# Scores' factor by exp(-2 ln) of the summed norms, with joined row and head copies, in an attention and expert kernel

## The chip, the cores and the metric

The kernel runs on one core of a Trainium2 chip. The metric is the device time of one execution in microseconds. Before the change it is 966.4 us in the median of three runs (966.29 to 967.87).

## The reference

The input is 32 sequences of 128 tokens with 256 features, and a context of the same shape. There are 16 heads of 16 features. After a layer norm, attention against the context comes with an unusual score, and then a second layer norm and a top-2 mixture of 8 experts with 1024 hidden features:

```python
scores = jnp.einsum('bhqd,bhkd->bhqk', qh, kh)
norm_q = jnp.linalg.norm(qh, axis=-1)
norm_k = jnp.linalg.norm(kh, axis=-1)
D_udps = (norm_q[..., :, None] + norm_k[..., None, :]) ** 2
D_safe = jnp.where(D_udps == 0.0, jnp.inf, D_udps)
scores = alpha * 4.0 * scores / D_safe
attn = jax.nn.softmax(scores, axis=-1)
...
logits = jnp.einsum('btd,de->bte', x, Wr)
w, idx = jax.lax.top_k(jax.nn.softmax(logits, axis=-1), 2)
h = jax.nn.gelu(jnp.einsum('btd,edh->ebth', x, W1) + b1[:, None, None, :], approximate=False)
y = jnp.einsum('ebth,ehd->ebtd', h, W2) + b2[:, None, None, :]
out = jnp.einsum('ebtd,bte->btd', y, dispatch)
```

For each query and key of each head the score is divided by the square of the sum of the two norms. With lq and lk the logarithms of the norms, and q', k' the unit vectors, 4 q.k / (nq + nk)^2 equals (q'.k') (1 - tanh^2((lq - lk) / 2)). The kernel before uses this form. The changed kernel computes exp(-2 ln((nq + nk) / scale)) and multiplies the raw q.k with it.

## The kernel before, in words

All five engines have programs written out by hand, with semaphores between them; no scheduler moves anything. Attention works on pairs of sequences, 16 pairs (`NP`). The loop of each engine is a software pipeline over `it`: while pair `it` gets its scores, pair `it + 1` is projected and its norms are made, pair `it + 2` is normalised, and pair `it - 1` is projected out and routed. Each pair has four factor steps n = 0 to 3: sequence b = n // 2 and half of the heads h = n % 2, so 8 heads, 1024 columns.

For one pair the work around the change is this:

1. TensorE projects q and k into a bank; ScalarE squares it (`squares`, L789) and copies it out (L792), then copies v (L781).
2. VectorE sums the squares over each head (L1060) and splits the sums in mantissa and exponent (`mantissas`, L1067 to L1070). ScalarE takes Ln (`norm_ln`, L796), VectorE forms the logarithm of the norms, with a sign, and splits it in three bf16 parts (`logarithms`, L1078 to L1092). ScalarE takes Exp (`norm_exp`, L800) and VectorE makes the unit vectors' coefficients (`unit_coefficients`, L1096 to L1102).
3. TensorE transposes the parts (`rows`, L433). VectorE copies them to `aq` and `kbr` (L1111, L1114), and SyncE writes the key rows by six small transfers into one row each of `uk` (`flat_rows`, L308).
4. POOL scales q and k to unit vectors (`units`, L1501, L1505), TensorE transposes them (`stack`) and ScalarE copies them out (L806, L809).
5. `factors(n)`: a matmul of `aq` and `uk` gives the sum for 128 x 1024 (L473), ScalarE applies Tanh (L817) and Square (L819). `scores(n)`: TensorE makes q.k (L485), VectorE multiplies by the factor (L1124) and takes the maximum (L1130).
6. `turned(n, i)`: TensorE transposes the product (L495) and subtracts the maximum by eight matmuls (L502), ScalarE takes the softmax's Exp (L827), and `values(n)` (L519) is the last step.

Three PSUM banks (`gen`) are handed round by the list `TURNS`: each use takes the bank that was used three places earlier, and waits until that use's reader has released it. So `wsum`, the sum of a weight's squares (L585, then L1283), takes the bank that the first exponential of n = 1 (`ex10`) has read, and `ex20` takes that of `wsum`. A factor's matmul needs that ScalarE has read the factor before, since there is one `u_ps`.

Meanwhile the expert weights are loaded and split (`weight_high` L862, `weight_low` L1277), and every second pair's tokens are routed and scattered (L1517). After the last pair come 71 slots of 128 tokens through the experts (L711, L928, L1375, L1377, L729).

ScalarE evaluates functions from a table that is loaded in sets. The build puts an instruction ACT_TABLE_LOAD ahead of an activation whose function is not in the set that is loaded; it is attributed to that activation's line.

Of the kernel before, what the change touches and what calls it, by code (L numbers as in the profile page):

```python
# [12 lines left out]
P = 128  # L13
# [19 lines left out]
QK_SCALE = 2.0 ** 12  # L33
# [7 lines left out]
    "dve_norms": ["mant", "ah", "parts", "coef"],  # L41
# [37 lines left out]
def build(nc, ctx, io):  # L79
# [119 lines left out]
    with ExitStack() as a:  # L199
# [19 lines left out]
        colscale = alloc(a, "colscale", [P, 2 * NH], F32)  # L219
        signs = alloc(a, "signs", [P, 2 * NH], F32)  # L220
# [11 lines left out]
        na = {k: alloc(a, f"na_{k}", [P, 2, 2 * NH], I32 if k in ("mant", "ex") else F32)  # L232
              for k in ("mant", "ex", "exf", "ln", "ah", "y", "y2", "n2y2", "rn", "coef", "r1", "r2")}
        ar = alloc(a, "ar", [P, 2, 2, RROWS], BF16)
        kbr = pair(a, "kbr", [RROWS, P], BF16)
# [3 lines left out]
        aq = pair(a, "aq", [RROWS + NSPLIT, P], BF16)  # L239
        uk = pair(a, "uk", [RROWS + NSPLIT, NH * P], BF16)  # L240
# [10 lines left out]
        wkk = alloc(a, "wkk", [P, 1], I32)  # L251
# [19 lines left out]
        def sync_program(sp):  # L271
# [125 lines left out]
        def tensor_program(pe):  # L397
# [49 lines left out]
            def stack(b, p):  # L447
                pe.wait_ge(*at("unit", p + 1))
# [13 lines left out]
            def factors(n, p):  # L462
# [300 lines left out]
        def scalar_program(act):  # L763
# [20 lines left out]
            def squares(b, p):  # L784
# [5 lines left out]
                if p:  # L790
                    act.wait_ge(*at("unit", p))
# [20 lines left out]
            def factors(n, p):  # L812
# [52 lines left out]
            for it in range(-1, NP + 3):  # L865
# [17 lines left out]
                if 0 <= it < NP:  # L883
                    norm_exp(it)
# [65 lines left out]
        def vector_program(dve):  # L950
# [31 lines left out]
            def set_scales():  # L982
# [10 lines left out]
                dve.tensor_scalar(escale[:, :], abig[:, :].bitcast(F32), QK_SCALE ** -2, None, ALU.mult).then_inc(sig("set_a"), 1)  # L993
                dve.memset(signs[:, 0:NH], 1.0)
# [645 lines left out]
```

## Time and profile before

| what | value |
|---|---|
| median of the runs | 966.4 us |
| the profiled execution, its own time | 970.74 us |
| its span on the core | 968.9 us |
| mean granted TensorE clock | 0.977 |
| PE busy, PEld busy | 898.1 us (93%), 789.8 us (82%) |
| DVE busy | 697.2 us (72%) |
| ACT busy | 634.5 us (65%) |
| POOL busy | 415.5 us (43%) |

PE is TensorE's matmuls, PEld its weight loads, DVE is VectorE, ACT is ScalarE, POOL is GpSimd, SP is SyncE. Idle is what a view puts ahead of an instruction, with the instruction that ended it behind an arrow. A group of the view by line has the number of instructions, their busy time in us, the mean of one in ns, and the idle time ahead of them. The granted clock is a share of TensorE's full 2.4 GHz, so 0.50 is 1.2 GHz. A stretch of time is given from the start of the span.

### The profile page before, as it was taken

The numbers are of one execution on the slowest core, as the hardware profiler recorded it, in microseconds if no ns is written. First come the engines' busy times: TensorE is split into PE (matmuls) and PEld (weight loads), VectorE is DVE, ScalarE is ACT, GpSimd is POOL, SyncE is SP. The second block draws the span as 40 slices with busy tenths as digits, with TensorE's granted clock in tenths as the row PEclk, the third lists the DMA queues.
The fourth block names the chain that finished last, engine by engine and source line by source line (L and its number), as shares of the span: only waits on it lengthen the run. The fifth ranks groups of instructions, "written<-read, shape, count | busy, mean of one in ns | idle before, by whom it ended". The sixth has DMA issues, their size and how long they took to land.

```text
span 968.9 us, 30634 instructions
## 1 busy us (share of the span) xinstructions
PE 898.1 (93%) x10701; PEld 789.8 (82%) x10701; DVE 697.2 (72%) x1833; ACT 634.5 (65%) x1236; POOL 415.5 (43%) x540
## 2 busy tenths in 40 slices
PE   3999999998999999989899699899999999999994
PEld 2788887787877877878777589799999999999993
DVE  7677888777987887779768577766666666666662
ACT  3688887787877877878857356455555455554551
POOL 6344456538546565385253532623222232222322
PEclk9799999999999999999979799999999999999998
DMA  5222122314132333253044773443333233332222
GB/s 150 70 72 89 41 83 80 112 41 128 57 99 76 126 123 103 92 171 111 20 139 134 275 273 52 85 93 52 51 52 51 47 52 52 52 51 48 46 30 22
DMA packets 61892, 84.82 MB, mean 88 GB/s; under 512 B 9872, under 2 KB 55312, under 8 KB 59568
## 3 DMA queue, kind: packets, MB, share of 16 engines
q1 hardware_dynamic: 47504, 64.26, 21.0%
q0 software_dynamic: 13296, 18.00, 11.1%
q8 instruction: 91, 1.49, 0.6%
q10 hardware_dynamic: 944, 0.60, 0.2%
q14 instruction: 57, 0.47, 0.2%
HBM read 49.86 MB, written 31.92 MB: 84 GB/s over the span
## 4 chain that ended last, share of the span: by engine, by line
PE 74%; issue 7%; DVE 6%; ACT 6%; POOL 3%; another core or an unknown queue 1%; DMA 1%; DVEq 0%; POOLq 0%; ACTq 0%
PE s_ps L711 10%; PE u_ps L711 10%; PE pv_ps L729 9%; PE gen L729 9%; PE gen L502 5%; PE gen L495 5%; PE s_ps L485 5%; PE u_ps L473 3%; PE pv_ps L519 2%; PE gen L544 2%; ACT pt L827 2%; PE gen L415 2%; PE gen L680 2%; PE gen L418 2%; PE gen L422 1%
## 5 line engine op out<-in xcount | busy, mean ns | idle before, releaser
L1567 POOL DMA_INDIRECT out<-yw,rb x71 | 110.3, 1553 | 269.4 <-DVE yw L1392 253.4
L928 ACT ACTIVATE h<-s_ps,b1t,inv 128x128 f32<-128x128 f32 x288 | 107.8, 457 | 89.6 <-PE s_ps L711 79.3
L928 ACT ACTIVATE h<-u_ps,b1t,inv 128x128 f32<-128x128 f32 x280 | 104.7, 459 | 87.4 <-PE u_ps L711 86.4
L1375 DVE TENSOR_SCALAR hs<-h,hsc 128x512 f16<-128x512 f32 x142 | 69.7, 491 | 120.4 <-ACT h L928 102.0
L827 ACT ACTIVATE pt<-gen,escale 128x512 f32<-128x512 f32 x128 | 86.8, 686 | 50.4 <-PE gen L502 34.5
L1377 DVE SCALAR_TENSOR_TENSOR hs<-h,hsc,hs 128x512 f16<-128x512 f32 x142 | 106.7, 751 | 5.1
L711 PE MATMUL s_ps<-xt,w1s 128*128 128x128 f16 x1728 | 104.8, 220 | 2.2 <-issue 2.2
L1517 POOL DMA_INDIRECT xrec<-rec,idx x64 | 77.8, 1215 | 60.9 <-DVE idx L1229 44.7
L711 PE MATMUL u_ps<-xt,w1s 128*128 128x128 f16 x1680 | 102.5, 220 | 0.9 <-issue 0.9
L711 PEld LDWEIGHTS s_ps<-xt,w1s 128*128 x1728 | 99.8, 99 | 2.8 <-issue 2.3
L729 PE MATMUL pv_ps<-w2s_sb,hs 128*128 x864 | 100.5, 272 | 0.5 <-issue 0.5
L711 PEld LDWEIGHTS u_ps<-xt,w1s 128*128 x1680 | 97.2, 99 | 2.0 <-issue 1.5
L1124 DVE SCALAR_TENSOR_TENSOR tw<-th,s_ps 128x1024 f32<-128x1024 f32 x64 | 77.9, 1217 | 27.2 <-PE s_ps L485 21.9
L729 PE MATMUL gen<-w2s_sb,hs 128*128 x840 | 97.4, 273 | 0.0
L729 PEld LDWEIGHTS pv_ps<-w2s_sb,hs 128*128 128x128 f16 x864 | 82.5, 98 | 11.0 <-issue 1.5
L495 PE MATMUL gen<-idf,tw 128*128 128x128 f32 x512 | 79.5, 278 | 10.7 <-DVE wcl L1283 7.9
L502 PE MATMUL gen<-negb,mhl 128*128 128x128 bf16 x1024 | 79.2, 220 | 9.7 <-POOL mhl L1488 9.3
L729 PEld LDWEIGHTS gen<-w2s_sb,hs 128*128 128x128 f16 x840 | 80.9, 98 | 8.8
L1130 DVE TENSOR_REDUCE tm<-tw 128x8 f32<-128x1024 f32 x64 | 78.1, 1220 | 2.2
L817 ACT ACTIVATE th<-u_ps 128x1024 f32<-128x1024 f32 x64 | 65.6, 1026 | 20.5 <-PE u_ps L473 20.3
L502 PEld LDWEIGHTS gen<-negb,mhl 128*128 128x128 bf16 x1024 | 67.9, 99 | 13.6 <-POOL mhl L1488 11.6
L485 PE MATMUL s_ps<-kt,qt 32*128 32x128 f32 x1024 | 75.6, 286 | 0.9 <-DVE tw L1124 0.9
(251 smaller groups left out, 1741.8 us busy)
## 6 DMA issues: line engine op xcount, KB each, us to landing
wl<-L_ffn_W SPq DMA_DIRECT2D x16, 1024.0 KB
rb<-xrec SPq DMA_DIRECT2D x71, 132.5 KB
w2s<-wst SPq DMA_DIRECT2D x8, 1024.0 KB
w2s_sb<-w2s SPq DMA_DIRECT2D x8, 1024.0 KB, 20.4
xin<-x SPq DMA_DIRECT2D x32, 128.0 KB, 3.5
cin<-ctx SPq DMA_DIRECT2D x32, 128.0 KB, 2.1
xres<-x SPq DMA_DIRECT2D x32, 128.0 KB
out<-x SPq DMA_DIRECT2D x30, 128.0 KB, 2.0
```

The lines of the kernel that those rows point to most:

```text
L485: ins = pe.matmul(s_ps[:, i, j * P:(j + 1) * P], qt[b][rws, j // 2, :], kt[b][rws, j // 2, j % 2, :], start=True, stop=True)
L495: pe.matmul(g[:, j * P:(j + 1) * P], tw[h][:, i, j, :], idf[:, :], is_transpose=True, start=(j == 0), stop=False)
L502: ins = pe.matmul(g[:, j * P:(j + 1) * P], m, negb[:, :], start=False, stop=(j == 3 and part == 1))
L711: ins = pe.matmul(hbank[n % HBANKS][:, o:o + SLOT], w, xt[s % 2][:, xp, k, :], start=(t == 0), stop=(t == len(terms) - 1))
L729: ins = pe.matmul(y, hs[s % 3][:, hp, m, :], w, start=(m == 0 and t == 0), stop=(m == HC - 1 and t == 2))
L827: act.activation(pt[n % 2][:, i, :], turn(f"ex{n}{i}", p)[:, :], ACT.Exp, scale=escale[:, :]).then_inc(sig(f"ex{n}{i}"), 1)
L928: ins = act.activation(h32[n % HBANKS][:, m % HB, :], hbank[n % HBANKS][:, o:o + SLOT], ACT.Gelu, scale=inv1[:, bass.ds(ex, 1)].bitcast(F3 ...
L1124: dve.scalar_tensor_tensor(tw[h][:, :, :, :].rearrange("p i j k -> p (i j k)"), th[h][:, :], -1.0, s_ps[:, :, :].rearrange("p i k -> p (i ...
L1130: dve.tensor_reduce(tm[h][:, :], tw[h][:, :, :, :].rearrange("p i j k -> p (i j) k"), AX.X, ALU.max).then_inc(sig(f"tm{n}"), 1)
L1377: dve.scalar_tensor_tensor(lo, h, scale, hi, ALU.mult, ALU.subtract).then_inc(sig("lo"), 1)
L1517: pool.indirect_dma_start(xrec_d[:, :], bass.IndirectOffsetOnAxis(ap=idx[:, i, t:t + 1], axis=0), rec[m % 2][:, t, :], None).then_inc(sig( ...
L1567: pool.indirect_dma_start(out[:, :], bass.IndirectOffsetOnAxis(ap=rb[j][:, D + NE:D + NE + 1], axis=0), yw[s % 2][:, :], None, compute_op= ...
```

## The change

The factor is made another way, and some copies are joined.

- `norm_ln` and `norm_exp` become `roots`: ScalarE takes Ln of the sums of squares with a small bias, and Exp of -0.5 times that right behind, which gives 1/norm. VectorE corrects it by a Newton step and forms the norm itself (`norms`), which it splits in three parts. Mantissas, signs and unit coefficients are gone.
- `factors`: Tanh becomes Ln (new line L822), and Square becomes Exp with scale -2 and a bias tile (L824).
- `units`: POOL multiplies q by a constant per head and copies k, with a wait for q and k alone and one signal for each sequence.
- `scores` on VectorE multiplies without the -1.
- `aq`, `kbr` and `uk` hold both sequences of a pair; two copies take the place of four, and one semaphore counts all six row transfers. The first factor of a pair waits for all six.
- `heads_back` makes one product instead of two, and `weight_exponent` writes in place.

The core of the diff:

```diff
@@ flat_rows (SP)
-                for b in range(2):
-                    sp.wait_ge(*at(f"rowk{b}", p + 1))
-                    if p:
-                        sp.wait_ge(*at(f"su{2 * b + 1}", p))
-                    for s in range(NSPLIT):
...
+                sp.wait_ge(*at("rowk", p + 1))
+                if p:
+                    sp.wait_ge(*at("u3", p))
+                for s in range(NSPLIT):
+                    for b in range(2):
...
@@ factors (PE)
-                pe.wait_ge(*at(f"rowq{b}", p + 1))
-                pe.wait_ge(*dma(f"flat{b}", NSPLIT * (p + 1)))
+                if n == 0:
+                    pe.wait_ge(*at("rowq", p + 1))
+                    pe.wait_ge(*dma("flat", 2 * NSPLIT * (p + 1)))
@@ scalar_program
-            def norm_ln(p):
-                act.wait_ge(*at("mant", p + 1))
-                act.activation(na["ln"][:, :, :], na["mant"][:, :, :].bitcast(F32), ACT.Ln).then_inc(sig("nln"), 1)
-
-            def norm_exp(p):
-                act.wait_ge(*at("ah", p + 1))
-                act.activation(na["y"][:, :, :], na["ah"][:, :, :], ACT.Exp, scale=-1.0).then_inc(sig("ny"), 1)
+            def roots(p):
+                for b in range(2):
+                    act.wait_ge(*at(f"n2{b}", p + 1))
...
+                act.activation(na["ln"][:, :, :], n2[:, :, :], ACT.Ln, bias=tiny[:, :]).then_inc(sig("nln"), 1)
+                act.wait_ge(*at("nln", p + 1))
+                act.activation(na["y"][:, :, :], na["ln"][:, :, :], ACT.Exp, scale=-0.5).then_inc(sig("ny"), 1)
...
-                act.activation(th[h][:, :], u_ps[:, :], ACT.Tanh, scale=0.5).then_inc(sig(f"th{n}"), 1)
+                act.activation(th[h][:, :], u_ps[:, :], ACT.Ln, scale=-0.5 / NORM_SCALE).then_inc(sig(f"th{n}"), 1)
                 act.wait_ge(*at(f"th{n}", p + 1))
-                act.activation(th[h][:, :], th[h][:, :], ACT.Square).then_inc(sig(f"t2{n}"), 1)
+                act.activation(th[h][:, :], th[h][:, :], ACT.Exp, scale=-2.0, bias=centre[:, :]).then_inc(sig(f"t2{n}"), 1)
@@ vector_program, norms (new; mantissas, logarithms, unit_coefficients are removed)
+            def norms(p):
+                dve.wait_ge(*at("ny", p + 1))
+                step(dve.tensor_tensor(na["y2"][:, :, :], na["y"][:, :, :], na["y"][:, :, :], ALU.mult))
+                step(dve.scalar_tensor_tensor(na["n2y2"][:, :, :], n2[:, :, :], TINY, na["y2"][:, :, :],
+                                              ALU.max, ALU.mult))
+                step(dve.scalar_tensor_tensor(na["rn"][:, :, :], na["n2y2"][:, :, :], -3.0, na["y"][:, :, :],
+                                              ALU.add, ALU.mult))
+                step(dve.scalar_tensor_tensor(na["r1"][:, :, :], n2[:, :, :], TINY, na["rn"][:, :, :],
+                                              ALU.max, ALU.mult))
...
@@ rows (DVE)
+                dve.tensor_copy(kbr[:, :, :], both[:, :, 1, :]).then_inc(sig("rowk"), 1)
...
+                dve.tensor_copy(aq[0:RROWS, :, :], both[:, :, 0, :]).then_inc(sig("rowq"), 1)
@@ scores (DVE)
-                dve.scalar_tensor_tensor(tw[h][:, :, :, :].rearrange("p i j k -> p (i j k)"), th[h][:, :], -1.0,
...
+                dve.tensor_tensor(tw[h][:, :, :, :].rearrange("p i j k -> p (i j k)"), th[h][:, :],
+                                  s_ps[:, :, :].rearrange("p i k -> p (i k)"), ALU.mult).then_inc(sig(f"tw{n}"), 1)
@@ units (POOL)
-                pool.wait_ge(*at("coef", p + 1))
...
+                pool.wait_ge(*at(f"qke{b}", p + 1))
...
+                pool.tensor_tensor(qu[b][:, :, :], qk[:, b, 0:NH, :],
+                                   colscale[:, :].unsqueeze(2).to_broadcast([P, NH, DK]), ALU.mult)
+                for odd in range(2):
+                    ins = pool.tensor_copy(ku[b][:, :, odd, :, odd, :],
+                                           qk[:, b, NH + odd:2 * NH:2, :].rearrange("p (k g) d -> p k g d", k=2))
@@ the orders
 ACT:   squares(0), v_out(0), roots (was norm_ln), turned(1, 0), [norm_exp], turned(1, 1)
 DVE:   squares(0), [mantissas], weight_diagonal, logits(0), norms (was logarithms), weight_exponent, [unit_coefficients], rows
```

On ACT, from the factors of n = 2 and 3 over the norms to the first softmax exponential of n = 1, the order is before (`th` is the factor, `pt` the exponentials, `vz` v, `na_ln` and `na_y` the norms' Ln and Exp):

```order
L817 ACTIVATE th<-u_ps 128x1024
L819 ACTIVATE th<-th 128x1024
L817 ACTIVATE th<-u_ps 128x1024
L819 ACTIVATE th<-th 128x1024
L789 ACTIVATE qk<-gen 128x512
L792 ACTIVATE qk<-gen 128x512
L781 ACTIVATE vz<-gen 128x16x16
L796 ACT_TABLE_LOAD
L796 ACTIVATE na_ln<-na_mant 128x64
L827 ACT_TABLE_LOAD
L827 ACTIVATE pt<-gen,escale 128x512
L800 ACTIVATE na_y<-na_ah 128x64
```

and from the factor of n = 3 on it is after:

```order
L822 ACT_TABLE_LOAD
L822 ACTIVATE th<-u_ps 128x1024
L824 ACT_TABLE_LOAD
L824 ACTIVATE th<-th,centre 128x1024
L791 ACTIVATE qk<-gen 128x512
L794 ACTIVATE qk<-gen 128x512
L783 ACTIVATE vz<-gen 128x16x16
L803 ACT_TABLE_LOAD
L803 ACTIVATE na_ln<-n,tiny 128x64
L805 ACT_TABLE_LOAD
L805 ACTIVATE na_y<-na_ln 128x64
L832 ACTIVATE pt<-gen,escale 128x512 x2
```

Each Ln and each Exp of a factor has a table load ahead of it, and the norms' Exp has moved ahead of the exponential. Over the whole program 36 table loads stand on ACT before, and 164 after.

On DVE, behind the sums of squares, the order is before (`wdg`, `wss` and `wcl` belong to the weight's exponent, `ar` are the three parts):

```order
L1266 TENSOR_TENSOR wdg<-gen,idf 128x128
L1270 TENSOR_REDUCE wss<-wdg 128x1
L1162 TENSOR_SCALAR r_l<-gen 128x8
L1078 SCALAR_TENSOR_TENSOR na_ah<-na_ln,na_exf 128x64
L1084 TENSOR_TENSOR na_r<-na_ah,signs 128x64
L1088 CAST ar<-na_r 128x4x16
L1089 TENSOR_TENSOR na_r<-na_r,ar 128x64
L1090 CAST ar<-na_r 128x4x16
L1091 TENSOR_TENSOR na_r<-na_r,ar 128x64
L1092 CAST ar<-na_r 128x4x16
L1283 TENSOR_SCALAR wcl<-gen 128x1
```

and after:

```order
L1242 TENSOR_TENSOR wdg<-gen,idf 128x128
L1246 TENSOR_REDUCE wss<-wdg 128x1
L1138 TENSOR_SCALAR r_l<-gen 128x8
L1067 TENSOR_TENSOR na_y<-na_y 128x64
L1068 SCALAR_TENSOR_TENSOR na_n2y<-n,na_y 128x64
L1070 SCALAR_TENSOR_TENSOR na_rn<-na_n2y,na_y 128x64
L1072 SCALAR_TENSOR_TENSOR na_r<-n,na_rn 128x64
L1078 CAST ar<-na_r 128x4x16
L1079 TENSOR_TENSOR na_r<-na_r,ar 128x64
L1080 CAST ar<-na_r 128x4x16
L1081 TENSOR_TENSOR na_r<-na_r,ar 128x64
L1082 CAST ar<-na_r 128x4x16
```

The chain from ScalarE's result to the last part has nine instructions instead of seven, and what it waits for is the Exp, not the Ln.

## Rows read from the trace of the kernel before

**Rows 1.** The page, part 1: busy time and its share of the span.
```profile
PE 898.1 (93%) x10701; PEld 789.8 (82%) x10701; DVE 697.2 (72%) x1833; ACT 634.5 (65%) x1236; POOL 415.5 (43%) x540
```

**Rows 2.** First and last pair, and pair 14: L817 in order of time.
```profile
31.06 1.02 ACT L817 ACTIVATE th<-u_ps 128x1024 f32<-128x1024 f32 x1 [0.26 <-PE u_ps L473]
...
481.98 1.02 ACT L817 ACTIVATE th<-u_ps 128x1024 f32<-128x1024 f32 x1 [0.64 <-PE u_ps L473]
...
493.04 1.02 ACT L817 ACTIVATE th<-u_ps 128x1024 f32<-128x1024 f32 x1 [0.32 <-PE u_ps L473]
...
513.77 1.04 ACT L817 ACTIVATE th<-u_ps 128x1024 f32<-128x1024 f32 x1
```

**Rows 3.** Stretch 166 to 463 us: PE, PEld, DVE, ACT, POOL, granted clock, DMA.
```profile
166.00:463.00 297.00, 278.85 (x3035) 233.07 (x3033) 239.31 (x705) 240.04 (x382) 173.16 (x260) 1.00 0.31 102
```

**Rows 4.** Waits, 166 to 463 us: total, times, longest.
```profile
...
ACT pt L827 <- remote: 14.4, 5, 2.9
...
ACT pt L827 <- PE gen L502: 13.7, 30, 1.2
...
ACT th L817 <- PE u_ps L473: 11.1, 19, 0.9
...
```

**Rows 5.** Groups of ACT: count | busy us, mean ns | idle before.
```profile
L827 ACT ACTIVATE pt<-gen,escale 128x512 f32<-128x512 f32 x128 | 86.8, 686 | 50.4 <-PE gen L502 34.5 <-remote 14.4
...
L819 ACT ACTIVATE th<-th 128x1024 f32<-128x1024 f32 x64 | 67.7, 1058 | 2.0
...
L796 ACT ACT_TABLE_LOAD x16 | 20.5, 1283 | 0.3
...
L827 ACT ACT_TABLE_LOAD x15 | 19.2, 1283 | 0.3
...
L834 ACT ACTIVATE osb<-pv_ps 128x512 f32<-128x512 f32 x32 | 19.1, 598 | 1.9 <-PE pv_ps L519 0.3
```

**Rows 6.** Order of time on ACT: start, duration, line, tiles, [idle before].
```profile
250.32 1.04 ACT L817 ACTIVATE th<-u_ps 128x1024 f32<-128x1024 f32 x1
...
261.35 1.02 ACT L817 ACTIVATE th<-u_ps 128x1024 f32<-128x1024 f32 x1
262.41 1.06 ACT L819 ACTIVATE th<-th 128x1024 f32<-128x1024 f32 x1
...
266.73 0.38 ACT L781 ACTIVATE vz<-gen 128x256 f32<-128x256 f32 x1
267.13 1.28 ACT L796 ACT_TABLE_LOAD   x1
268.43 0.26 ACT L796 ACTIVATE na_ln<-na_mant 128x64 f32<-128x64 f32 x1
268.70 1.28 ACT L827 ACT_TABLE_LOAD   x1
270.00 0.69 ACT L827 ACTIVATE pt<-gen,escale 128x512 f32<-128x512 f32 x1
...
272.10 0.69 ACT L827 ACTIVATE pt<-gen,escale 128x512 f32<-128x512 f32 x1 [1.18 <-PE gen L502]
```

**Rows 7.** Groups of DVE and PE that stand in the norms' chain.
```profile
L1102 DVE TENSOR_TENSOR na_coef<-na_rn,colscale 128x64 f32<-128x64 f32 x16 | 3.6, 225 | 0.5
...
L585 PE MATMUL gen<-wss,ones_f 128*128 128x1 f32 x32 | 6.1, 260 | 4.8 <-ACT pt L827 3.1 <-issue 1.7
```

**Rows 8.** The SP queue: issues of six row copies of one pair.
```profile
243.49 3.67 SPq L308 DMA_DIRECT2D uk<-kbr  x6
```

**Rows 9.** PE after its idle times, in order of time.
```profile
24.96 0.66 PE L433 MATMUL gen<-idb,ar 128*96 128x128 bf16 x4 [4.09 <-DVE ar L1092]
...
40.48 1.49 PE L485 MATMUL s_ps<-kt,qt 32*128 32x128 f32 x16 [0.95 <-DVE tw L1124]
```

**Rows 10.** Stretches of 3 us: PE busy first, granted clock after POOL.
```profile
27.00:30.00 3.00, 3.00 (x14) 2.40 (x13) 1.90 (x7) 1.15 (x3) 1.57 (x4) 0.50 0.04 7
...
42.00:45.00 3.00, 3.00 (x9) 2.04 (x9) 2.44 (x2) 2.00 (x2) 0.45 (x3) 0.57 0.00 0
```

More of the change, by code:

```diff
@@ L32 @@
 X_SCALE = 2.0 ** 11
-QK_SCALE = 2.0 ** 12
+TINY = 1e-37
+NORM_SCALE = 4.0
+CENTRE = 2.0
 ONE = 1 << 23
@@ L231, in build @@
         n2 = alloc(a, "n2", [P, 2, 2 * NH], F32)
[L232 to L233 removed]
+        na = {k: alloc(a, f"na_{k}", [P, 2, 2 * NH], F32)
+              for k in ("ln", "y", "y2", "n2y2", "rn", "r1", "r2")}
         ar = alloc(a, "ar", [P, 2, 2, RROWS], BF16)
[L235 removed]
+        kbr = alloc(a, "kbr", [RROWS, 2, P], BF16)
         qt, kt = pair(a, "qt", [P, 2, P], F32), pair(a, "kt", [P, 2, 2, P], F32)
[L239 to L240 removed]
+        aq = alloc(a, "aq", [RROWS + NSPLIT, 2, P], BF16)
+        uk = alloc(a, "uk", [RROWS + NSPLIT, 2, NH * P], BF16)
         vz = pair(a, "vz", [P, 2, NH, VC], F32)
@@ L447, in stack @@
             def stack(b, p):
-                pe.wait_ge(*at("unit", p + 1))
+                pe.wait_ge(*at(f"un{b}", p + 1))
                 g = pe_turn(pe, f"qte{b}", p)
@@ L1090, in logarithms @@
+                step(dve.tensor_tensor(v4(na["r2"]), v4(na["r1"]), part(0), ALU.subtract))
                 step(dve.tensor_copy(part(1), v4(na["r2"])))
[L1091 to L1103 removed]
@@ L1105, in rows @@
-            def rows(p):
-                gb = turn("rows_t", p)[:, :].bitcast(BF16)
-                dve.wait_ge(*at("rows_t", p + 1))
-                for b in range(2):
-                    if p:
-                        dve.wait_ge(*at(f"su{2 * b + 1}", p))
-                    dve.tensor_copy(aq[b][0:RROWS, :], gb[0:RROWS, 2 * b * P:(2 * b + 1) * P]).then_inc(sig(f"rowq{b}"), 1)
-                    if p:
-                        dve.wait_ge(*dma(f"flat{b}", NSPLIT * p))
-                    dve.tensor_copy(kbr[b][:, :], gb[0:RROWS, (2 * b + 1) * P:(2 * b + 2) * P]).then_inc(sig(f"rowk{b}"), 1)
+                step(dve.tensor_tensor(v4(na["r1"]), v4(na["r2"]), part(1), ALU.subtract))
@@ new lines, in norms, with rows @@
+                dve.tensor_copy(part(2), v4(na["r1"])).then_inc(sig("parts"), 1)
+            def rows(p):
+                gb = turn("rows_t", p)[:, :].bitcast(BF16)[:, 0:4 * P]
+                dve.wait_ge(*at("rows_t", p + 1))
+                both = gb[0:RROWS, :].rearrange("r (b i t) -> r b i t", b=2, i=2)[:, :, :, :]
+                if p:
+                    dve.wait_ge(*dma("flat", 2 * NSPLIT * p))
+                dve.tensor_copy(kbr[:, :, :], both[:, :, 1, :]).then_inc(sig("rowk"), 1)
+                if p:
+                    dve.wait_ge(*at("u3", p))
+                dve.tensor_copy(aq[0:RROWS, :, :], both[:, :, 0, :]).then_inc(sig("rowq"), 1)
@@ L1284, in weight_exponent @@
                 dve.wait_ge(*at("wcl", p + 1))
-                exponent(wcl[:, :], wkk[:, :])
-                dve.tensor_copy(dst[:, p % NE:p % NE + 1], wkk[:, :])
-                dve.tensor_scalar(wsc[:, :], wkk[:, :], -float(ONE), 268.0 * ONE, ALU.mult, ALU.add).then_inc(sig("wsc"), 1)
+                place = dst[:, p % NE:p % NE + 1]
+                exponent(wcl[:, :], place)
+                dve.tensor_scalar(wsc[:, :], place, -float(ONE), 268.0 * ONE, ALU.mult, ALU.add).then_inc(sig("wsc"), 1)
             for it in range(-2, NP + 3):
@@ L1325, in vector_program @@
                 if 0 <= it + 1 < NP:
-                    logarithms(it + 1)
+                    norms(it + 1)
                 if 0 <= it < NP:
```

117 lines of the change are left out of this document (36 added, 81 removed), and 2 rows, old and new, of the table TURNS.

## The prediction

> **What bounds the kernel now.** I read the page's busy line first: TensorE (PE) is busy for 93% of the span [rows 1], but that is a mean over two stages, attention over 16 pairs and then the experts, and the change touches only attention. So next a window over the middle of attention. Two L817 rows frame the stage: the first factor of the first pair starts at 31.06 us and that of the last at 513.77 [rows 2], so 15 pairs take 482.7 us, 32.2 each. In the window of 297 us PE is busy 278.9, ScalarE (ACT) 240.0, VectorE (DVE) 239.3, GpSimd (POOL) 173.2 [rows 3]. Per pair of 32.3 us in that window (9.2 pairs) that is PE 30.3, ACT 26.1, DVE 26.0. PE paces, and ACT is second with only 6.2 us of idle per pair. Then the waits of ACT: it waits on PE in small pieces, 13.7 us in 30 pieces before the softmax exponentials, 11.1 us in 19 before the factors, and 14.4 us in 5 pieces of up to 2.9 that the trace puts to an unnamed releaser [rows 4]. ACT and PE run in lockstep, each waiting a little for the other; what is added to ACT beyond some 4 to 6 us a pair must lengthen the pair.
>
> **The change, part by part.** *Table loads.* This decides. The built order shows an ACT_TABLE_LOAD ahead of every Ln and every Exp that alternate. Before, Tanh, Square and Exp follow one another with none, and only the norms' Ln is framed by two. Now each of the four factors of a pair has two (one ahead of Ln, one ahead of Exp), and the norms keep two: 10 a pair where there were 2. Over the program 164 stand where 36 did, 128 more. One takes 1283 ns, each of the 31 in the two groups of the attention stage alike [rows 5]. What one adds to the queue is a little more. From vz at 266.73 to the exponential at 270.00 are 3.27 us with two loads and one 0.26 us Ln in between [rows 6]; without loads, with engines' overlap, I put these starts 0.43 apart, so 1.42 per load where it breaks an overlap. Tanh to Square, which depends on it, stands 1.06 apart (261.35, 262.41) for 1.02 of work [rows 6], so no overlap is lost there: 1.30. Per pair 4 x 1.42 + 4 x 1.30 = 10.9 us.
>
> The Trainium skill (ScalarE: Activation LUTs, What ACT_TABLE_LOAD costs) says that a switch costs the 1283 ns load and about 1380 ns of drain, some 2.66 us in total. By that page the 128 loads would add 340 us and the time would be near 1290. The row disagrees: Ln starts 1.30 us after its load [rows 6], so the load's length agrees and the drain is not there to be seen.
>
> *Activations.* Tanh becomes Ln with the same shape, Square becomes Exp; I charge equal time, as nothing in the rows separates functions. But the new Exp reads its bias from a tile. 128x512 with a per-partition operand takes 686 ns (L827), the same size without one 598 (L834) [rows 5]: 0.09 more. Five such per pair (four Exp, the norms' Ln) make 0.4. So ACT gets 11.3 us more a pair: 26.1 + 11.3 = 37.4, above PE's 30.3. ACT becomes the engine that paces.
>
> *What ACT still waits for.* Waits that come from PE being late vanish, since PE works through the 2.6 us that each factor now takes longer. Round trips stay. After the norms' Exp comes the first exponential of factor 1, then PE's weight sum (its bank is freed by just that exponential), eight matmuls and the second. Today the two start 2.10 apart (270.00, 272.10) [rows 6] with small work between that moves away: about 1.5 idle. In every second pair the unnamed wait of 2.9 stands in its place [rows 4], 0.8 more on the mean. Four later hand-overs keep some 0.8 in all (estimated from the 13.7 us in 30 pieces), two new small ones, ahead of factor 1 and ahead of factor 2's exponentials, 0.6. Sum 3.7, and 37.4 + 3.7 = 41.1 us a pair.
>
> *TensorE's clock.* PE will idle 10 us a pair. The longest piece is new: PE finishes the projection and waits with the weight products for ACT to empty the q k bank behind factors 2 and 3, about 4 us. In this trace PE idle for 4.09 us ahead of 24.96 [rows 9] is followed by a granted clock of 0.50, that is 1.2 of 2.4 GHz, while PE is fully busy [rows 10]; after a wait of 0.95 at 40.48 [rows 9] it falls as well, to a mean of 0.57 [rows 10]. Cold, the scores, values and transposes behind the wait double: between nothing (hidden behind the norms' loads) and 2.9 us a pair (weight products 0.9, scores 1.1 and values 0.6 are hidden in part, two groups of 0.9 are not). I take 0.9. Pair: 42.0 us.
>
> *The norms on DVE.* Removed are three mantissa steps, the sum, the sign and the unit coefficient; added are the clamped ones. The part that leads to the row copies grows from seven to nine instructions of 225 ns [rows 7] and now starts after two loads instead of one. Both stand in the shadow of the round trip just counted; where the cover is gone they cost at most 0.5 + 1.5 a pair. The wait that is added on DVE (for the norms' Exp) has the weight exponent, the row copies and factor 3's product queued behind it, and PE waits for the exponent to free a bank: 0.3 of the 0.6 above is that. Ahead of the first pair nothing covers it: +1.9 once.
>
> *POOL, joined copies, joined products.* POOL no longer waits for coefficients; it has 13 us of slack a pair [rows 3], and stack is early by that but waits for a bank anyway: 0. Two DVE copies in place of four, one product in place of two, one copy less in the weight exponent: between 0 and -0.6 a pair, on an engine off the path: 0. The new product of factor and scores keeps its 1024 columns: 0. The first factor now waits for all six row transfers instead of three; six are issued in 3.67 us, done at 247.16 [rows 8], while that pair's first factor runs at 250.32 [rows 6]: 0, and 1.8 if that cover went (half of the 3.67).
>
> **The sum.** 15 pairs at 42.0 are 630; the first four have no routing work and are 0.8 shorter each, 627. Against 482.7: +144. The last pair has its eight loads and 0.4 of bias, less 2.4 of waits that vanish: +8.5. Start +1.9. In pair 14 factor 2 runs 11.1 after factor 1 (481.98 to 493.04) [rows 2] where others need 4.5, while DVE makes tables; with ACT pacing I count 4 of that back. The expert stage has the same instructions: 0. Total +151, on the profiled execution's 970.7 (span 968.9) 1121; that execution is 4.3 above the median of 966.4, so 1117. As the waits are the weaker part and my estimates of them are rounded upward, I forecast **1115**.
>
> **The rivals.**
> *ACT's idle swallows it.* Nearly all waits go, 1.5 a pair left, and the clock costs nothing: 38.9 a pair, 583 + 7, +108: 1075. For it: 6.2 idle per pair today, all waits on PE. Against it: the round trip through the weight sum cannot be filled, as ACT's order is fixed.
> *The clock falls in each pair at the worst place.* 2.9 a pair instead of 0.9: +30 more, and if DVE's cover goes as well, another 0.5 a pair: about 1150. For it: the 0.95 us wait was already followed by the lower clock. Against: the clock is 1.00 over the whole window of today, its PE idle of 2 us a pair (18.1 of 297 us) notwithstanding [rows 3].
> *The loads do not appear: not slower.* Mechanism: Ln and Exp served by one set, so that the loads at the norms go too. ACT then loses 2 x 1.42 and gains 0.4, 23.7 a pair; PE's 30.3 is the floor, so at most 1.9 x 15 = 28 us are gained: about 940 to 955. It decides if the profile after has fewer than 36 loads. Against it: the built order shows all 164. The Trainium skill (ScalarE: Activation LUTs, Table sets: the hidden batching unit) states such a set, natural_log_exp_and_others, and one load for Ln then Exp; the trace of before has separate loads for Ln and Exp [rows 6], which speaks for two sets here too.
> *Each switch costs the drain as well* (from 128 x 2.7, about 1290): 1%; the start of Ln right behind its load excludes it.
>
> **How the numbers follow.** Forecast with its own range 1095 to 1130: 0.64. Swallowed, 1060 to 1095: 0.17. Clock and more, 1130 to 1165: 0.15. No loads, 940 to 955: 0.03. Drain: 0.01. The range that leaves out no more than 2 in 10 is 1080 to 1140. Its low end is nearly the floor without clock, its high end the forecast with about 1.7 a pair more. A difference of 0.2% (1.9 us) can be told here. Faster 0.025, within 0.005, slower 0.97.
>
> **What would show it.** 164 ACT_TABLE_LOAD of 1283 ns; ACT busy near 37 us a pair, idle under 5, PE at 30 busy of 40 to 42; first factor of the last pair near 31 + 2 + 627 = 660; th pairs, L822 to L824, 2.3 apart; dips of PEclk in attention; the end of the span some 455 us after the last pair's first factor, as now. Wrong would be: a pair under 38.9 (waits), over 44 (clock or DVE's chain), table loads that are shorter or missing, or Ln over 1024 columns unlike Tanh's 1.02.

## The result, and the profile after

| | time, us | ratio to before | 95% interval |
|---|---|---|---|
| before | 967.0 (966.3 to 967.9) | | |
| changed | 1121.7 (1118.8 to 1124.2) | 1.160 | 1.157 to 1.163 |

The change makes the kernel 154.7 us slower. The forecast was 1115, with a range of 1080 to 1140. The profiled execution took 1123.9 us, with a span of 1122.1.

The page of the changed kernel, part 1 and the line of the granted clock in part 2 (tenths, in 40 slices):

```profile
PE 966.5 (86%) x10701; PEld 839.9 (75%) x10701; DVE 679.4 (61%) x1672; ACT 802.9 (72%) x1364; POOL 407.8 (36%) x540
...
PEclk8688998998988998998988988899999999999998
```

TensorE falls from 93% to 86% of a longer span [rows 1], and ScalarE goes from 634.5 us busy to 802.9, which is 168.4 more. 128 loads of 1.283 us are 164.2 of that. The clock line has an 8 or less in about every second slice of the attention stage, its first 25 slices. Next the groups of ScalarE, which answer to [rows 5]:

```profile
L832 ACT ACTIVATE pt<-gen,escale 128x512 f32<-128x512 f32 x128 | 85.5, 681 | 70.5 <-PE gen L504 69.1
L822 ACT ACT_TABLE_LOAD x64 | 82.1, 1283 | 1.1
L824 ACT ACT_TABLE_LOAD x64 | 82.1, 1283 | 1.1
L824 ACT ACTIVATE th<-th,centre 128x1024 f32<-128x1024 f32 x64 | 73.5, 1148 | 0.8
L822 ACT ACTIVATE th<-u_ps 128x1024 f32<-128x1024 f32 x64 | 65.5, 1024 | 0.7
L803 ACT ACT_TABLE_LOAD x16 | 20.5, 1283 | 0.3
L805 ACT ACT_TABLE_LOAD x16 | 20.5, 1283 | 0.3
...
L803 ACT ACTIVATE na_ln<-n,tiny 128x64 f32<-128x64 f32 x16 | 5.6, 347 | 0.2
```

Every load takes the 1283 ns of before. Ln over 1024 columns takes 1024 ns where Tanh took 1.02 us; Exp with its bias tile takes 1148 where Square took 1058, 0.09 more. The norms' Ln takes 347 with its bias tile and took 0.26 us without one ([rows 6]), the same 0.09. The first factor of the first pair and that of the last pair, which answer to [rows 2]:

```profile
31.97 1.02 ACT L822 ACTIVATE th<-u_ps 128x1024 f32<-128x1024 f32 x1
```
```profile
660.66 1.02 ACT L822 ACTIVATE th<-u_ps 128x1024 f32<-128x1024 f32 x1
```

15 pairs take 628.7 us instead of 482.7, that is 41.9 a pair instead of 32.2. This is 146.0 of the 153.2 us by which the span is longer. Ahead of them 0.9 are lost (the start moves from 31.06 to 31.97), behind them 6.3 (from the last pair's first factor to the end it was 455.1 us and is 461.4).

One pair of ScalarE in order of time, from the factor of n = 2 on, to be laid beside [rows 6]:

```profile
378.57 1.28 ACT L822 ACT_TABLE_LOAD   x1
379.86 1.02 ACT L822 ACTIVATE th<-u_ps 128x1024 f32<-128x1024 f32 x1
380.90 1.28 ACT L824 ACT_TABLE_LOAD   x1
382.20 1.15 ACT L824 ACTIVATE th<-th,centre 128x1024 f32<-128x1024 f32 x1
383.36 1.28 ACT L822 ACT_TABLE_LOAD   x1
384.66 1.02 ACT L822 ACTIVATE th<-u_ps 128x1024 f32<-128x1024 f32 x1
385.70 1.28 ACT L824 ACT_TABLE_LOAD   x1
386.99 1.15 ACT L824 ACTIVATE th<-th,centre 128x1024 f32<-128x1024 f32 x1
388.05 0.58 ACT L791 ACTIVATE qk<-gen 128x512 f32<-128x512 f32 x1
388.52 0.59 ACT L794 ACTIVATE qk<-gen 128x512 f32<-128x512 f32 x1
389.00 0.38 ACT L783 ACTIVATE vz<-gen 128x256 f32<-128x256 f32 x1
389.40 1.28 ACT L803 ACT_TABLE_LOAD   x1
390.70 0.35 ACT L803 ACTIVATE na_ln<-n,tiny 128x64 f32<-128x64 f32 x1
391.06 1.28 ACT L805 ACT_TABLE_LOAD   x1
392.36 0.26 ACT L805 ACTIVATE na_y<-na_ln 128x64 f32<-128x64 f32 x1
392.52 0.67 ACT L832 ACTIVATE pt<-gen,escale 128x512 f32<-128x512 f32 x1
396.81 0.69 ACT L832 ACTIVATE pt<-gen,escale 128x512 f32<-128x512 f32 x1 [3.62 <-PE gen L504]
```

From the first load to the end of v the engine never waits. Ln to Exp is 2.34 us here (379.86 to 382.20), where Tanh to Square was 1.06; the factor of n = 2 to that of n = 3 is 4.80 where it was 2.41 (261.35 to 263.76). The one long wait is the last row: 3.62 us ahead of the second exponential of n = 1, where it was 1.18, or 2.9 in pairs with routing. What TensorE does meanwhile:

```profile
389.25 1.44 PE L581 MATMUL gen<-wl 128*128 128x128 bf16 x16 [4.02 <-ACT qk L794]
...
391.38 2.08 PE L487 MATMUL s_ps<-kt,qt 32*128 32x128 f32 x16
393.39 1.08 PE L521 MATMUL pv_ps<-pt,vz 128*32 128x128 f32 x16
...
394.85 1.09 PE L497 MATMUL gen<-idf,tw 128*128 128x128 f32 x4
395.74 1.03 PE L504 MATMUL gen<-negb,mhl 128*128 128x128 bf16 x8
```

and the stretches of 3 us around it (PE, PEld, DVE, ACT and POOL busy, then the granted clock):

```profile
386.00:389.00 3.00, 0.00 (x0) 0.00 (x0) 0.34 (x1) 2.99 (x4) 2.02 (x4) 1.00 0.82 258
389.00:392.00 3.00, 2.75 (x26) 2.75 (x28) 1.09 (x4) 2.95 (x5) 2.67 (x6) 0.63 0.27 96
392.00:395.00 3.00, 3.00 (x33) 2.36 (x32) 1.93 (x9) 1.18 (x3) 0.69 (x3) 0.50 0.00 0
395.00:398.00 3.00, 3.00 (x30) 2.87 (x30) 0.78 (x5) 1.19 (x4) 0.00 (x0) 0.73 0.00 0
```

TensorE idles for 4.02 us until ScalarE has copied q and k out (`qk`, L794), which it does only after the factors of n = 2 and 3. Then the granted clock falls to 0.50, 1.2 GHz, while it works: the scores take 2.08 us where they take 1.16 at the full clock, and ScalarE gets what its second exponential reads (L497 and L504, from 394.85 on) late. Over the window of [rows 3] the clock was 1.00 and is 0.90:

```profile
166.00:463.00 297.00, 245.31 (x2323) 201.26 (x2321) 175.86 (x471) 257.71 (x350) 126.35 (x195) 0.90 0.22 71
```

ScalarE is busy for 257.7 of 297 us, 36.4 of the 41.9 of a pair; TensorE for 245.3. The idle time of 4.02 us stands in 12 of the 16 pairs, and in each of them the clock behind it is 0.50.

### The profile page after: what moved, and what is told of

Read it like the earlier page. It is cut to its first block, busy times and chain, and to the rows that moved or that the text cites. A ratio compares the mean times of both kernels' runs of the same rounds, so it can differ in the third digit from the quotient of the medians.

```text
span 1122.1 us, 30493 instructions
## 1 busy us (share of the span) xinstructions
PE 966.5 (86%) x10701; PEld 839.9 (75%) x10701; DVE 679.4 (61%) x1672; ACT 802.9 (72%) x1364; POOL 407.8 (36%) x540
## 4 chain that ended last, share of the span: by engine, by line
PE 56%; ACT 23%; issue 12%; DVE 5%; POOL 1%; DMA 1%; SPq 0%; DVEq 0%; ACTq 0%; POOLq 0%
PE s_ps L713 8%; PE u_ps L713 8%; PE pv_ps L731 8%; PE gen L731 8%; ACT L822 7%; ACT th L822 5%; PE gen L497 4%; PE gen L504 4%; ACT th L824 3%; PE pv_ps L521 3%; PE s_ps L487 3%; PE gen L581 2%; ACT pt L832 2%; DVE tw L1103 1%; PE gen L682 1%
## 5 line engine op out<-in xcount | busy, mean ns | idle before, releaser
L1103 DVE TENSOR_TENSOR tw<-th,s_ps 128x1024 f32<-128x1024 f32 x64 | 77.9, 1218 | 106.4 <-ACT th L824 99.5
L1460 POOL CAST mhl<-tm 128x8 bf16<-128x8 f32 x64 | 12.1, 189 | 269.8 <-DVE tm L1108 269.6
L713 PE MATMUL u_ps<-xt,w1s 128*128 128x128 f16 x1680 | 99.8, 219 | 0.3 <-issue 0.3
L487 PE MATMUL s_ps<-kt,qt 32*128 32x128 f32 x1024 | 88.9, 321 | 3.9 <-DVE tw L1103 3.9
L497 PE MATMUL gen<-idf,tw 128*128 128x128 f32 x512 | 90.5, 306 | 1.2 <-DVE tw L1103 0.8
L504 PE MATMUL gen<-negb,mhl 128*128 128x128 bf16 x1024 | 89.1, 237 | 2.1 <-POOL mhl L1462 1.8
L731 PEld LDWEIGHTS pv_ps<-w2s_sb,hs 128*128 128x128 f16 x864 | 82.4, 98 | 11.3 <-issue 1.5
L487 PEld LDWEIGHTS s_ps<-kt,qt 32*128 32x128 f32 x1024 | 75.0, 220 | 15.0 <-issue 12.9
L824 ACT ACT_TABLE_LOAD x64 | 82.1, 1283 | 1.1
```

The lines of the kernel that those rows point to most:

```text
L487: ins = pe.matmul(s_ps[:, i, j * P:(j + 1) * P], qt[b][rws, j // 2, :], kt[b][rws, j // 2, j % 2, :], start=True, stop=True)
L497: pe.matmul(g[:, j * P:(j + 1) * P], tw[h][:, i, j, :], idf[:, :], is_transpose=True, start=(j == 0), stop=False)
L504: ins = pe.matmul(g[:, j * P:(j + 1) * P], m, negb[:, :], start=False, stop=(j == 3 and part == 1))
L713: ins = pe.matmul(hbank[n % HBANKS][:, o:o + SLOT], w, xt[s % 2][:, xp, k, :], start=(t == 0), stop=(t == len(terms) - 1))
L731: ins = pe.matmul(y, hs[s % 3][:, hp, m, :], w, start=(m == 0 and t == 0), stop=(m == HC - 1 and t == 2))
L824: act.activation(th[h][:, :], th[h][:, :], ACT.Exp, scale=-2.0, bias=centre[:, :]).then_inc(sig(f"t2{n}"), 1)
```

## The experiments

Ratios are to the kernel before on the same chip. The first four kernels ran on one chip (before 966.8 us) and the next four on a second (966.7). The last four ran on a third, where the kernel before takes 956.4 us (before_8loads_warm, one_set_pool) and 954.8 us (the other two); their times aren't to be laid beside those of the first eight without that difference. Pairs with routing are every second pair from the fifth on; the others are called pairs without routing.

| kernel | table loads | time, us | ratio | 95% interval |
|---|---|---|---|---|
| one_set | 4 | 966.7 | 1.0005 | 0.998 to 1.003 |
| before_8loads | 164 | 1115.3 | 1.154 | 1.151 to 1.158 |
| before_4loads | 100 | 1002.8 | 1.036 | 1.033 to 1.040 |
| after_warm | 164 | 1099.0 | 1.138 | 1.134 to 1.143 |
| one_set_scatter | 4 | 969.1 | 1.003 | 1.000 to 1.006 |
| before_scatter | 36 | 969.0 | 1.002 | 1.000 to 1.004 |
| one_set_split | 4 | 964.8 | 0.998 | 0.996 to 0.9996 |
| one_set_both | 4 | 967.6 | 1.0015 | 0.999 to 1.004 |
| before_8loads_warm | 164 | 1082.5 | 1.133 | 1.131 to 1.134 |
| one_set_pool | 4 | 943.2 | 0.986 | 0.9845 to 0.988 |
| one_set_split_again | 4 | 947.8 | 0.994 | 0.9925 to 0.995 |
| before_pool | 36 | 953.7 | 0.999 | 0.997 to 1.001 |

### The changed kernel without its table loads: one_set

```diff
         def scalar_program(act):
+            act.preload_act_table_set("natural_log_exp_and_others")
```

> The changed kernel with one line more: ahead of all of ScalarE's work the set natural_log_exp_and_others is loaded, so that Ln and Exp find their table in place; the built order has 4 table loads instead of 164. Theory 1 (the loads alone are the cost, and what else was changed is worth a few us): ACT loses 10 loads of 1.3 to 1.42 us a pair, TensorE paces again with 30.3 us busy of 31 to 32.5, the pair takes 31.0 to 32.5, the time is 940 to 975, point 950. Theory 2 (a part of the cost is the longer chain of the norms, the Exp with a bias tile and the joined row transfers): 985 or more. By the Trainium skill (ScalarE: Activation LUTs, Table sets: the hidden batching unit) the set serves both functions; that sentence also gives the 4 loads.

The built order has 4 loads, none of them inside a pair. The time is that of the kernel before: 966.7, ratio 1.0005. So 154.7 us hang on one line, and all of the rest of the change together is worth nothing that the time shows here. Theory 2 (985 or more) is out; the point of 950 was wrong too. The set that the Trainium skill names (ScalarE: Activation LUTs, Table sets: the hidden batching unit) does serve Ln and Exp. The trace agrees: four loads in all, and none between Ln and Exp or at the copies and squares between them. The build does not choose it by itself: in the changed kernel it puts a load at every alternation of Ln and Exp, and only with the common set in place does it leave these out.

Why not 950? The window of [rows 3] once more, of one_set, and the waits in it that bear on this:

```profile
166.00:463.00 297.00, 280.02 (x3035) 233.86 (x3035) 227.72 (x611) 219.96 (x364) 169.82 (x265) 0.99 0.32 102
```
```profile
ACT pt L833 <- remote: 26.0, 5, 5.3
...
ACT pt L833 <- PE gen L504: 22.2, 31, 3.2
...
DVE wcl L1260 <- remote: 10.7, 5, 2.2
```

ScalarE falls to 220.0 us busy, but TensorE stays at 280.0. ScalarE just waits longer at the same places: ahead of the second exponential of n = 1 it waits 3.2 us in pairs without routing (1.18 before) and 5.1 to 5.3 in pairs with routing (2.9 before), which is why the sum of the unnamed wait grows from 14.4 us [rows 4] to 26.0. Pairs without routing do become shorter, 30.43 us where they took 30.85, but those with routing take 33.9 to 35.5 where they took 33.8 to 34.0.

### The same loads in the kernel before: before_8loads and before_4loads

```diff
+                act.preload_act_table_set("exp_and_others")
                 act.activation(th[h][:, :], u_ps[:, :], ACT.Tanh, scale=0.5).then_inc(sig(f"th{n}"), 1)
                 act.wait_ge(*at(f"th{n}", p + 1))
+                act.preload_act_table_set("exp_and_others")
                 act.activation(th[h][:, :], th[h][:, :], ACT.Square).then_inc(sig(f"t2{n}"), 1)
```

before_4loads has the second of the two lines alone.

> The kernel before with one table load ahead of each Tanh and one ahead of each Square, of the set that is loaded already, and nothing else: 164 loads, as in the changed kernel, in the same eight places a pair. Theory 1: the pair takes 41 to 41.5 us where the changed kernel takes 41.9, since the bias tiles (0.4) and the later norms are missing; time 1105 to 1118, point 1110. Theory 2: under 1095. A third theory, that a load of the set that is already in place costs less than a switch, would show as loads shorter than 1283 ns and a time under 1050.

> The kernel before with a table load ahead of each Square alone: 100 loads, four more a pair, 5.2 us of ACT. It asks for the shape between none and eight. If ACT's idle of 6.2 us a pair swallowed loads first and the rest then came at full price: 966 to 980. If most waits of ACT are round trips that do not shrink, as the sum for eight loads assumed (9.7 of 11.3 surfaced): four loads cost 3 to 4.5 a pair, time 1012 to 1040, point 1020.

Eight loads a pair, of a set that is in place already, make the kernel before nearly as slow as the changed one: 1115.3, where 1110 was expected. The 6.3 us that are left to 1121.7 have about the size of the five operands from a tile, 0.45 us a pair (15 x 0.45 = 6.8), but no run took these out alone. A load of the set in place takes no less:

```profile
L817 ACT ACT_TABLE_LOAD x64 | 82.1, 1283 | 7.6 <-PE u_ps L473 6.8
L820 ACT ACT_TABLE_LOAD x64 | 82.1, 1283 | 1.3
```

Four loads cost 36.0 us, less than the 54 that I expected at the point and under the range of 1012 to 1040; the other reading, 966 to 980, is out as well. The next four cost 112.5. In pairs, by the first factors of the first and the last one: 32.2 us without, 34.6 with four (+2.4 for 5.2 us of loads), 41.4 with eight (+9.2 for 10.9, priced as in the prediction). About half of the first four went into ScalarE's idle time; the second four cost 6.8 for 5.7, more than they last. The half is a mean of two kinds of pair: without routing the four cost 2.9 us (30.85 to 33.78), with routing 0.8 in most (33.85 to 34.6 or 34.7), and there the unnamed wait is gone. The granted clock over the window of [rows 3] is still 1.00 with four loads (TensorE's wait for q and k is 1.8 us there), and 0.90 with eight (3.7 to 3.8 us):

```profile
166.00:463.00 297.00, 265.78 (x2834) 219.54 (x2832) 224.44 (x647) 267.66 (x394) 170.87 (x248) 1.00 0.30 98
```
```profile
166.00:463.00 297.00, 247.20 (x2343) 202.71 (x2341) 184.94 (x541) 257.50 (x352) 134.44 (x199) 0.90 0.22 72
```

### TensorE kept busy: after_warm and before_8loads_warm

```diff
                     turned(1, 0, it)
+                    if it < NP - 1:
+                        pe.wait_ge(*at("tw2", it + 1))
+                    for _ in range(16 if it < NP - 1 else 0):
+                        pe.matmul(s_ps[:, 0, :], ones_b[0:RROWS, :], bqp[:, :], start=True, stop=True)
                     weight_products(it)
```

> The changed kernel with 16 idle matmuls of 512 columns (0.22 us each at the full clock) on TensorE, behind the transposes of factor 1 and ahead of the weight products, where TensorE idles 4.0 us in each pair and the granted clock then falls to 0.50 for some 7 us. They write a bank that the next scores overwrite. If the clock costs what lies behind the idle time (scores, values and the transposes end 2.3 us later): the clock stays at 1.00, the pair falls by 1.5 to 2.3, time 1087 to 1100. If the chain of the norms on ACT and DVE is as late as TensorE, so that a warm clock gives little: 1110 or more. My own 0.9 a pair in the prediction would be 1108.

> before_8loads with the 16 idle matmuls of after_warm at the same place. Four loads a pair cost 36 us, eight 148: the second four cost three times the first. Theory K (clock): part of the second four's price is the granted clock that falls once TensorE waits 4 us in each pair; with it held the time falls by 18 to 30 us, as between the changed kernel and after_warm (23 us): 1085 to 1097, and the second four then cost some 85, about their own 5.4 us a pair. Theory L (the loads push a chain other than ACT's own): under 8 us, 1107 or more.

Work that computes nothing makes the changed kernel 22.7 us faster (1121.7 to 1099.0, within the expected 1087 to 1100); its ratio falls from 1.160 to 1.138. The place of the idle time, with the filler in it (L634), and the stretches of 3 us around it:

```profile
366.39 3.62 PE L634 MATMUL s_ps<-bqp,ones_b 96*128 96x512 bf16 x16
370.57 1.08 PE L581 MATMUL gen<-wl 128*128 128x128 bf16 x16 [0.56 <-ACT qk L798]
...
371.98 1.16 PE L487 MATMUL s_ps<-kt,qt 32*128 32x128 f32 x16
```
```profile
375.92 0.69 ACT L836 ACTIVATE pt<-gen,escale 128x512 f32<-128x512 f32 x1 [1.42 <-PE gen L504]
```
```profile
366.00:369.00 3.00, 3.00 (x22) 1.57 (x21) 1.17 (x1) 2.97 (x3) 1.08 (x3) 1.00 0.69 199
369.00:372.00 3.00, 2.44 (x27) 1.71 (x25) 0.69 (x1) 2.98 (x5) 2.36 (x4) 1.00 0.43 153
372.00:375.00 3.00, 2.15 (x37) 1.76 (x37) 1.55 (x7) 2.47 (x5) 2.00 (x6) 1.00 0.12 45
```

The clock stays at 1.00 there, the scores take 1.16 us instead of 2.08, and ScalarE's wait ahead of the second exponential of n = 1 falls to 1.3 to 2.3 us in the pairs of the window, where it was 3.1 to 4.1. Over 205 to 574 us the clock is 0.97, where the changed kernel has 0.90. A pair takes 39.8 instead of 41.9 us. The same filler brings before_8loads from a ratio of 1.154 to 1.133, and from 41.4 to 39.4 us a pair on another chip; the clock over the window of [rows 3] is then 0.98. Theory K holds for both. With the clock held, the second four loads cost 4.8 us a pair in the traces (34.6 to 39.4), 5.3 by the medians and 6.2 by the ratios (1.036 to 1.133 of 966.8 us, over 15 pairs), for 5.7 us of queue time. The two kernels ran on different chips, so this is no closer than that; it is about the full price, and the price above full went with the clock.

### The unnamed wait: one_set_scatter, before_scatter and one_set_both

```diff
                 if 0 <= it - 3 < NP - 1 and it % 2 == 0:
-                    scatter(2, 1, it - 3)
-                    scatter(3, 0, it - 3)
-                    scatter(3, 1, it - 3)
...
                 if 0 <= it < NP:
                     split_max(3, it)
+                if 0 <= it - 3 < NP - 1 and it % 2 == 0:
+                    scatter(2, 1, it - 3)
+                    scatter(3, 0, it - 3)
+                    scatter(3, 1, it - 3)
```

> one_set with the last three record scatters of every second pair (L1490 there) moved on GpSimd from ahead of the units to behind the maximum of factor 3. In one_set, as in the kernel before, TensorE's weight sum is recorded at 301.07, but VectorE and ScalarE, which wait for it and for the transposes behind it, go on only at 304.32 and 304.44, 0.85 us after the last of these scatters ends (303.48). Theory A: the hand-over is held while GpSimd issues these transfers; moved away, the 2.1 us unnamed wait of 7 pairs goes: 950 to 955, point 952. Theory B: the coincidence says nothing and the wait is that of something else in pairs with routing: unchanged, 963 to 968. Theory C: the hold moves with the scatters to the transposes of factor 3: 962 to 970 and the unnamed wait at another line.

> The kernel before with the same three scatters moved. Theory A: the unnamed wait of 2.6 us in every second pair goes, of which 1.2 to 1.6 stay as the usual round trip: 7 x 1.4, 955 to 959. Theory B or C: 964 to 969. Against one_set_scatter it also prices the change itself with its table loads gone: theory 1 (loads alone) says the two lie within 5 us.

> one_set with both edits, the moved scatters and the split transfers. If the two are independent: the sum of their gains. Point 951 (theory A, join worth nothing), 946 if the join is worth 0.4 a pair, 966 if neither does anything.

Nothing was gained: 969.1 and 969.0, ratios of 1.003 and 1.002, and with the split transfers of the next section beside them 967.6 (one_set_both) against 964.8 without the moved scatters. In one_set_scatter the unnamed wait of ScalarE falls from 26.0 to 11.3 us and that of VectorE ahead of `wcl` goes. But the 11.3 stand at a new place, ahead of the pair's last exponential, where the scatters now run, and behind it TensorE waits for that exponential with the heads' transposes (L536):

```profile
PEld gen L536 <- ACT pt L833: 11.8, 5, 2.4
ACT pt L833 <- remote: 11.3, 5, 2.3
```

```profile
319.18 0.69 ACT L833 ACTIVATE pt<-gen,escale 128x512 f32<-128x512 f32 x1 [2.25 <-remote]
```

At the old place the wait is now 3.3 us, put to TensorE, where it was 5.3: so what is held there is 2.0 us, and not the whole 5.3. At both places the engine that waited goes on 0.84 us behind the end of the last scatter (303.48 to VectorE's 304.32 in one_set, 318.34 to 319.18 here). That is theory C: the hold goes with the scatters. What it is the trace doesn't say.

### The joined row transfers: one_set_split, and again

```diff
-                for s in range(NSPLIT):
-                    for b in range(2):
+                for b in range(2):
+                    for s in range(NSPLIT):
...
-                        sp.dma_start(dst, kbr[s * STRIP:s * STRIP + NH, b, :]).then_inc(sig("flat"), 16)
+                        sp.dma_start(dst, kbr[s * STRIP:s * STRIP + NH, b, :]).then_inc(sig(f"flat{b}"), 16)
```

and the waits for them on TensorE and VectorE accordingly.

> one_set with the six row transfers issued sequence by sequence on two semaphores, so that the first factor of a pair again waits for three of them and not for six. In the prediction this join was priced at 0, and at most 1.8 us a pair without cover. With TensorE pacing again, the cover is as in the kernel before (last issue done 3.2 us ahead of ScalarE's first factor): 0, 963 to 968. If the join delays TensorE's first factor by even 0.4 us a pair: 958 to 961.

> one_set_split once more, since one_set_pool ran on another chip, where the kernel before takes 956.4 and not 966.7 us and where the unnamed wait of the routed pairs is absent from the trace of one_set_pool. If the chip is like that one (before near 956): theory S (the exchange on GpSimd is worth what it was priced, 4.5 us) expects a ratio of 0.990 to 0.992; theory U (nearly all of the 1.4% is that the change with its loads gone is faster once the unnamed wait is absent) 0.985 to 0.988. On a chip like the first ones (before near 967): 0.996 to 1.000 again.

964.8 against one_set's 966.7, on another chip: the join costs at most some 2 us, and the ratios' intervals (0.998 to 1.003, 0.996 to 0.9996) overlap. On one chip, one_set_scatter and one_set_both differ by the split alone and lie 1.5 us apart (969.1 and 967.6), within their spread. The price of 0 stands. On the third chip the same kernel has a ratio of 0.994, above both ranges that were expected (0.990 to 0.992 and 0.985 to 0.988), and there the unnamed wait is missing from the traces of all four kernels. The pairs ahead of the first routing take 30.05 us in this kernel and 30.46 in before_pool. So what is left of the change without its loads gains some 0.4 us in a pair without routing, and 0.2 to 0.6% in all where the six transfers are split.

### One exchange on GpSimd: one_set_pool and before_pool

```diff
-                if 0 <= it - 2 < NP - 1:
-                    record_low(0, it - 2)
                 if 0 <= it < NP:
                     split_max(0, it)
+                if 0 <= it - 2 < NP - 1:
+                    record_low(0, it - 2)
```

> one_set_split with one exchange on GpSimd: the maximum of factor 0 is split (0.2 + 0.2 us) ahead of the low half of the record (0.65), not behind it. TensorE waits for it in routed pairs, 1.4 to 1.7 us in 4 of 9 pairs. If GpSimd is late there by its own queue: 7 x 0.65 = 4.5 us, 958 to 962. If what is late is the scatter ahead of it in the queue, the exchange helps by the same amount; if the wait then goes to VectorE's x1 or to the bank: 963 to 966.

> The kernel before with the exchange of one_set_pool alone (factor 0's maximum split ahead of the record's low half). Theory S: 7 routed pairs by 0.65, a ratio of 0.995 (4.5 us). If the exchange does nothing here: 1.000. If it removed the unnamed wait by itself: 0.985 to 0.99.

one_set_pool is the fastest kernel of this study: 943.2 us where the kernel before takes 956.4, a ratio of 0.986. It beats both kernels. Against one_set_split_again (947.8, the same chip, another session) that is 4.6 us by the times and 7.4 by the ratios; 4.5 were priced. By the traces a pair with routing takes 31.0 us instead of 31.65, which over 7 such pairs is 4.5. TensorE's wait for the split maximum, 5.7 us in 4 of the window's pairs there, is 3.2 here:

```profile
PE gen L504 <- POOL mhl L1464: 5.7, 4, 1.4
```
```profile
PE gen L504 <- POOL mhl L1464: 3.2, 4, 0.8
```

In the kernel before TensorE's wait falls to 3.1 us as well, but the exchange gives a ratio of 0.999 with an interval that holds 1 and not the 0.995 of theory S, so it is not shown to help by itself.

## Why the prediction was right

**The count and the price of the loads** carried it. 164 loads of 1283 ns; one of them lengthens the distance of two functions by 1.28 us (2.34 instead of 1.06). one_set takes them out and the whole cost goes; before_8loads puts eight a pair in and all but 6 us come. Against the rule of 2.66 us a switch (the Trainium skill, ScalarE: Activation LUTs, What ACT_TABLE_LOAD costs), Ln starts 0.01 us behind its load's end at 379.86, and the load starts 0.02 behind the activation ahead of it; the measurement decides for 1.3. The figure of 1290 in the prediction doesn't follow from the 340 us beside it: 966 and 340 are 1306, and it takes the forecast of 1115 and 128 drains of 1.38 us (177) to come to 1292.

**The operands from a tile** were sized right on ScalarE, 0.09 each, 0.45 a pair; what they alone cost in time is not shown.

**The pair** was put at 42.0 us and is 41.9, the last pair's first factor at 660 and is at 660.7. But the two parts of that sum were both off and balanced each other, which is luck. ScalarE's work was put at 37.4 and is 36.4, its waits at 3.7 + 0.9 and they are 5.5. Part of the first is the price of 1.42 that four of the loads were given: over the whole program ScalarE's busy time rises by 168.4 us, 10.5 a pair and not 11.3.

**The waits.** The unnamed wait in every second pair, 0.8 on the mean, did not come back: no wait of that kind is in the changed kernel's window. That the scatters now end while ScalarE works through factors 2 and 3 and the norms, when nobody waits, is my reading of it; no run tried it. It fits that the last scatter of such a pair ends at 390.54, while the first exponential starts at 392.52. The wait ahead of the second exponential of n = 1, priced at 1.5 us, is 3.1 to 4.1 in the seven pairs of the window, 3.7 on the mean. With the filler it is 1.3 to 2.3, so the round trip had about the right price, and what came on top is the clock.

**The clock** was the term that was mis-sized. It was put at 0.9 us a pair for lack of a row at the place itself, with bounds of 0 and 2.9. The filler gives 2.1 in the profiled executions (31 us of 15 pairs) and 22.7 us of the medians, so 1.5 to 2.1 a pair. The mechanism was right, down to the idle time of 4 us behind the q k bank, and it happens in 12 of the 16 pairs.

**Start, end, pair 14.** The start cost 0.9 instead of 1.9, the end 6.3 instead of 8.5 (the terms named for it, 10.9 and 0.4 less 2.4, make 8.9). In pair 14 the factor of n = 2 now comes 7.4 us behind that of n = 1, where other pairs need 6.8: the stall of 6.5 us that VectorE's tables made has gone nearly whole, where I gave back 4.

**The edits priced at nothing** (norms, joined copies, joined products, units on GpSimd) are together worth less than 0.5% in one_set, as priced; on the third chip they gain 0.6%, with the row transfers split again. The longer chain of the norms is in all of these kernels and was not tried alone.

**The rival "the loads do not appear"** failed for the changed kernel, but its mechanism is real: with one line the loads go. Its time of 940 to 955 was too low on the first chips (966.7). It let all of ScalarE's relief reach the pair, up to 1.9 us; a pair without routing gained 0.4 and one with routing nothing.

## What to carry to other kernels

Before a function on ScalarE is exchanged for another, count the table loads in the built order, per turn of the loop: an Ln and an Exp that alternate cost 1.3 us at each change unless the common set is loaded first, and then they cost nothing. What is added to an engine that isn't the pacing one can be partly free while it has idle time (here 2.8 of 5.2 us), and can then cost more than its length when TensorE's waits grow so long that its granted clock falls (here 6.8 for 5.7 us, with a wait of 3.8). If TensorE must wait some 4 us, work that computes nothing can be faster than waiting: 22.7 us here.

## What the runs showed of the hardware that I had not expected

- A table load of the set that is already in place takes the same 1283 ns (before_8loads, 128 of them).
- TensorE's granted clock falls after 4.0 us of idle in 12 of the 16 pairs of the changed kernel: 0.50 for some 7 us (389.8 to 396.7 in the pair shown). That it would fall there was forecast as possible; that it costs 1.5 to 2.1 us a pair was not.
- Hand-overs from TensorE are held in pairs in which GpSimd issues record scatters, by some 1.7 us in the kernel before (2.9 instead of 1.18) and 2.0 in one_set (5.3 instead of 3.3), on two of three chips. The hold moves with the scatters. On the third chip it is absent from the traces, and the kernel before is 1.1% faster there. Its cause stays open.
